# A decoder kernel on one core: raw scores that run ahead, moved between the scores of two pairs of heads

## The reference, cut to what matters

```python
# layer 0: head width 8 (weights ternary, inputs quantised, rotary left out here)
att = jnp.einsum('bhnr,bhmr->bhnm', ql, kl) / math.sqrt(dk)
y = jax.nn.softmax(att, axis=-1) @ v
# layer 2: head width 8
scores = jnp.einsum('bnhr,bmhr->bhnm', Qr, Kr) / math.sqrt(RANK)
A = jax.nn.softmax(scores, axis=-1)
out = jnp.einsum('bhnm,bmhv->bnhv', A, V).reshape(b, n, d)
# layer 3, first attention of its cross block: head width 32, masked after the softmax
a = jax.nn.softmax(jnp.einsum('bhsd,bhtd->bhst', q, k) * D ** (-0.5), axis=-1)
mask = (jnp.arange(t)[None, :] > jnp.arange(s)[:, None]).astype(a.dtype)
o = jnp.einsum('bhst,bhtd->bhsd', a * mask, v)
```

## Time and profile before

| | |
|---|---|
| median of 3 runs | 1848.97 us (1846.86 to 1850.07) |
| the profiled execution | 1849.52 us, its span 1846.9 us |
| PE busy | 1549.2 us (84%) |
| DVE busy | 1040.8 us (56%) |
| ACT busy | 643.8 us (35%) |
| POOL busy | 211.0 us (11%) |
| rounds of layer 0's attention, 79.66 to 178.70 | PE 94.72, DVE 76.94, ACT 64.52 busy of 99.04 us, clock 0.96 |
| rounds of layer 2's attention, 1007.85 to 1104.30 | PE 92.13, DVE 76.89, ACT 64.64 of 96.45 us, clock 1.00 |
| rounds of layer 3's attention, 1518.13 to 1648.30 | PE 124.72, DVE 84.44, ACT 70.55, POOL 46.50 of 130.17 us, clock 1.00 |

### The profile page before, as it was taken

One profiled execution on the slowest core, in us unless ns is written; L12 is line 12 of the kernel. 1 busy time (PEld: TensorE's weight loads), 2 busy tenths in 40 slices (PEclk: granted clock), 3 DMA queues, 4 the chain that ended last, 5 costly groups with the idle time before them and its releaser, 6 DMA issues. The chain is left out here.

```text
span 1846.9 us, 22396 instructions
## 1 busy us (share of the span) xinstructions
PE 1549.2 (84%) x8280; PEld 707.8 (38%) x8280; DVE 1040.8 (56%) x2589; ACT 643.8 (35%) x926; POOL 211.0 (11%) x227
## 2 busy tenths in 40 slices
PE   1798689995677999988989998988988679996986
PEld 0332344442233344446433333353446423344343
DVE  4696445447945677753444962535445457734444
ACT  1366242214324033333424663412221255542431
POOL 2000010001000524331000000000000103321000
PEclk9899689996979889998998997997996789997798
DMA  4000000002000000000020000000010000000000
GB/s 200 0 1 1 1 1 0 1 26 108 1 0 1 17 29 2 1 1 1 1 88 13 1 1 0 1 1 1 1 68 1 1 0 1 2 1 1 1 1 12
DMA packets 4075, 27.16 MB, mean 15 GB/s; under 512 B 384, under 2 KB 2432, under 8 KB 2944
## 3 DMA queue, kind: packets, MB, share of 16 engines
q1 hardware_dynamic: 2912, 25.22, 3.4%
q10 hardware_dynamic: 1056, 0.52, 0.1%
HBM read 25.21 MB, written 0.52 MB: 14 GB/s over the span
## 5 line engine op out<-in xcount | busy, mean ns | idle before, releaser
L792 DVE TENSOR_REDUCE maxima<-banks 128x1 f32<-128x512 f32 (+4 forms) x640 | 362.7, 603 | 103.5 <-PE banks L647 96.4
L929 ACT ACTIVATE big<-banks 128x1024 f32<-128x1024 f32 (+2 forms) x320 | 294.3, 960 | 262.4 <-PE banks L690 94.1
L675 PE MATMUL banks<-big 32*128 32x512 f32 (+6 forms) x1280 | 230.3, 607 | 17.0 <-DVE big L813 12.6
L647 PE MATMUL banks<-big 32*128 32x77 bf16 (+6 forms) x1024 | 157.4, 293 | 22.9 <-ACT big L238 6.1
L1390 DVE TENSOR_TENSOR big<-big,banks 128x512 f32<-128x512 f32 (+1 forms) x116 | 79.7, 687 | 151.5 <-PE banks L1303 146.1
L711 PE MATMUL banks<-big,v_heads 128*9 128x512 f32 (+7 forms) x1024 | 158.6, 565 | 6.3 <-ACT heads_out L852 3.2
L446 POOL TENSOR_TENSOR rstd<-mean_var,minus_half 128x4 f32<-128x4 f32 x34 | 34.5, 1014 | 1078.8 <-DVE mean_var L346 1078.8
L1365 ACT ACTIVATE big<-banks 128x512 f32<-128x512 f32 (+1 forms) x116 | 69.1, 596 | 178.1 <-PE banks L1302 178.0
L647 PEld LDWEIGHTS banks<-big 32*128 32x128 bf16 (+1 forms) x1024 | 57.1, 97 | 177.3 <-DVE maxima L792 90.8
L1333 PE MATMUL banks<-big,moe_weights 128*128 128x512 f32 (+1 forms) x232 | 118.9, 597 | 3.0 <-ACT big L1373 2.6
L336 DVE BATCH_NORM_STATS2 stats<-banks 128x6 f32<-128x128 f32 x128 | 28.5, 284 | 135.6 <-PE banks L324 135.6
(11 more groups left out here) (409 smaller groups left out, 2254.6 us busy)
## 6 DMA issues: line engine op xcount, KB each, us to landing
moe_weights<-in_moe SPq DMA_DIRECT2D x1, 4864.0 KB, 14.9
moe_weights<-in_moe SPq DMA_DIRECT2D x1, 4768.0 KB, 22.0
moe_weights<-in_moe SPq DMA_DIRECT2D x1, 3264.0 KB, 10.5
moe_weights<-in_l3x SPq DMA_DIRECT2D x1, 3072.0 KB, 10.0
late_weights<-in_l2x SPq DMA_DIRECT2D x1, 2048.0 KB, 8.0
moe_weights<-in_l SPq DMA_DIRECT2D x1, 1234.0 KB, 13.1
rows<-in_rows SPq DMA_DIRECT2D x1, 1152.0 KB, 8.0
late_weights<-in_turned SPq DMA_DIRECT2D x1, 1152.0 KB, 17.3
```

What stands on the lines that cost most here:

```text
L647: last = nc.tensor.matmul(RING[n % NR][:, x * klen:x * klen + last_key(t)], q[rows, t * P:(t + 1) * P], ks[rows, 0:last_key(t)], start=Tru ...
L675: last = nc.tensor.matmul(SC[pair % 2][0:size, j % 2, n0:S], ks[rows, i * P:i * P + size], q[rows, n0:S], start=True, stop=turned)
L792: nc.vector.tensor_reduce(dst, src, AX_X, ALU.max).then_inc(ring_free.up(), 1)
L929: nc.scalar.activation(E[pair % NEP][0:size, :, n0:S], SC[pair % 2][0:size, :, n0:S], ACT.Exp, scale=scale).then_inc(exp_ready.up(), 1)
```

## The change

`scores` can now issue one pair alone, and where there are two pairs and more than one key tile, raws 0 and 1 stand between pair A's scores and pair B's. Everything else keeps its place.

```diff
--- before.py
+++ after.py
@@ -660,14 +660,15 @@
             last = nc.tensor.transpose(to[:, t * P:(t + 1) * P], negmax_tile, unit[:])
         last.then_inc(ring_ready.up(), 1)
 
-    def scores(pe, r):
+    def scores(pe, r, half=None):
         g, i = r // nkt, tile(r)
         b, k = groups[g]
         size, n0 = key_tiles[i], start(i)
         q, ks = queries(b, k), keys(b, k)
         if r % nkt == 0:
             pe.wait_ge(ring_free.sem, ring_free.at(maxima_turned[g] + 1))
-        for j in range(HB):
+        heads = range(HB) if half is None else range(2 * half, 2 * half + 2)
+        for j in heads:
             pair = r * pairs + j // 2
             if j % 2 == 0 and pair >= 2:
                 pe.wait_ge(exp_ready.sem, exp_ready.at(pair - 1))
@@ -675,7 +676,7 @@
             last = nc.tensor.matmul(SC[pair % 2][0:size, j % 2, n0:S], ks[rows, i * P:i * P + size], q[rows, n0:S], start=True, stop=turned)
             if turned and j % 2:
                 last.then_inc(score_ready.up(), 1)
-        for j in range(0 if turned else HB):
+        for j in () if turned else heads:
             pair = r * pairs + j // 2
             rows = slice(W * j, W * j + W)
             last = nc.tensor.matmul(SC[pair % 2][0:size, j % 2, n0:S], c.pick[rows, 4 // HB * j, 0:size], c.NMT[rows, g % 2, n0:S],
@@ -880,12 +881,15 @@
                 pe.wait_ge(project_free.sem, project_free.at(len(projections)))
             for r in range(R + later):
                 soon, rest = ahead(r)
+                between = pairs == 2 and nkt > 1
                 if r < R:
-                    scores(pe, r)
+                    scores(pe, r, 0 if between else None)
                 turn_first = mask == "causal" and next_group(r) is not None
                 if not turn_first:
                     for u in soon:
                         raw_scores(pe, u)
+                if r < R and between:
+                    scores(pe, r, 1)
                 if 0 <= r - 1 < R:
                     values(pe, r - 1)
                 if next_group(r) is not None:
```

## The result

The changed kernel took 1896.95 us, the median of four executions (1890.91 to 1898.54); the kernel before, measured beside it, 1848.54 (1846.86 to 1850.07). The ratio is 1.0256, with a 95% interval of 1.0231 to 1.0281: slower by 48.4 us, where 46.2 were forecast. The profiled execution is the lowest of the four, 1890.91 us with a span of 1888.0.

The account below looks back on a forecast made before the run. The prediction took the matmul engine's in-order chain, from pair A through pair B to the values, as the bound. Row-8 stages 28.4 plus layer 3 17.8 gave 46.2 us more, 1895.2 us, range 1877 to 1908.

Parts of the forecast that it names:

- The wait and its length: Row-8 rounds: pair B can't start before raw 1's weight load, 0.61, 1.18, 1.18 and 1.34 us after pair A.
- Values pass it on in full: Row-8 group: each delay of pair B reaches the values and the next round undiminished, 2.13 us a group, 14.49 for 12.36.
- 9.2 us less: Row-8 stages: lower bound if unseen slack swallowed the short delays of rounds 0 and 1, 14 x 0.66.
- Layer 3: Self-attention with a ring of two banks: rounds longer by 0.24, 0.85, 0.62 and 0.86 us, 17.8 in all.
- Ring banks: Longer rounds: reductions don't gate them, since banks for raws 2 and 3 are free earlier than wanted.
- Strict order: Rival, chance 0.14: pair B starts only with the held raws before it in PE's queue; 9.2 us more, 1904.4.
- the sum that hung on it, 55.4: Loss in us over the three stages instead of 46.2, if matmuls start and end strictly in program order.
- No hold: Rival, chance 0.06: pair B's products pass a raw waiting for its bank, so pair B starts as now; 1849 us.
- The repeated wait: The only instruction added, a wait already met; the forecast gave it no cost.
- took every group for a steady one: The sum applied one steady group's delays to all rounds with raws ahead: 28.4 us row-8, 17.8 layer 3.
- The place behind pair B costs the raws nothing: Old order: raws wait for pair A's rows, 0.96 us, longer than pair B's wait; gain booked at 0.
- the "faster" rival: Rival, chance 0.04: the vector engine is fed earlier in the row-8 stages, up to 14.0 us won, 1835.

Follow-up runs that it names:

- wait_only: Kernel before, order kept; ahead of pair B's first product PE waits for the bank raw 1 will take: 1893.37 us, 1.0259.
- no_repeat: Changed kernel without the repeated wait for the turned maxima ahead of pair B in a group's first round: 1893.42 us, 1.0246.
- after_again: The changed kernel run and profiled once more, nothing altered: 1898.33 us, 1.0267 against the kernel before.
- raw0_row8: Against the changed kernel: only raw 0 between the pairs, raw 1 behind pair B, and this in the row-8 stages alone: 1859.48 us, 1.0056.
- row8_only: Against the kernel before: the new order in the two row-8 stages alone, not in layer 3: 1880.12 us, 1.0182.
- l3_only: Against the kernel before: the new order in layer 3's first attention alone: 1865.73 us, 1.0106.
- raw0_between: Against the changed kernel: only raw 0 between the pairs, raw 1 behind pair B, in all three stages: 1862.20 us, 1.0075.

## Why the prediction was right

**The wait and its length.** The central step was that pair B can't start before raw 1's weight load, 1.18, 1.18 and 1.34 us after pair A in three rounds of four. The profile after has 1.17, 1.18 and 1.34, and wait_only pays the same with the wait alone (47.7 us in its stages, against 48.0 and 46.0).

**Values pass it on in full.** In a steady group this holds. The four rounds of a row-8 group got longer by 0.48, 0.27, 0.74 and 0.73 us; the forecast was 0.38, 0.28, 0.74 and 0.73. The group took 14.58 us where 14.49 was forecast. Nothing was swallowed by slack there, for which the prediction had named 9.2 us less.

**Layer 3.** The rounds got longer by 0.18, 0.97, 0.64 and 0.86; the forecast was 0.24, 0.85, 0.62 and 0.86. The stage lost 17.5 us for 17.8.

**Ring banks.** That the reductions would not gate the longer rounds holds in this group: the weights of raws 2 and 3 load at 127.20, 130.42 and 134.22, within 0.01 us of pair A's start. DVE's busy time stayed (11.33 us before, 11.26 after) and its share fell.

**Strict order.** This rival is wrong. In the first round the first two passes of pair B start ahead of the raws that stand before them in the queue: the row of six at 124.46, the raws at 125.43. Had pair B started with the raws, it would have been 0.97 behind pair A and the group some 0.36 us longer than forecast; the first round was 0.10 longer than forecast, and for another reason (below). By the Trainium skill (TensorE: Matmul & The Clock Gate, Part 3, "The mechanism") matmuls are in program order in start and in end; for starts this trace doesn't agree, here as in the earlier trace rows, and the sum that hung on it, 55.4, didn't come.

**No hold.** Wrong too: in the three rounds of this group in which raw 1 waits, pair B's loads come 0 to 0.01 us behind raw 1's, never ahead.

**What was mis-sized.** The repeated wait was booked as nothing. It costs 0.1 us in the first round of each group, on the path there because pair B decides: 0.7 us over the seven groups of a stage, some 2 us in all. no_repeat shows 2.1 (43.9 in the stages against 46.0). In the forecast of the group this is the whole difference between 14.49 and 14.58.

**What cancelled it.** The sum also took every group for a steady one. The first isn't: in layer 2's stage (after_again) its rounds got longer by 0, 0.14, 0.73 and 0.49 us, 1.37 in all, where the forecast had 2.13. In layer 3 the first two groups lost 1.90 and 2.45 us, where the steady ones lost 2.65 and the forecast had 2.57. Without the repeated wait, in no_repeat, the stages lost 43.9 us, so the forecast of 46.2 for that same mechanism was 2.3 too high. A term put at nothing and a term put too high, some 2 us each, met in 46.0: that is luck.

**What was overlooked.** "The place behind pair B costs the raws nothing" is right for their start and wrong for their report. In the kernel before, in the round of the earlier trace rows whose raws start at 134.34:

```profile
134.34 0.61 PE L647 MATMUL banks<-big 32*128 32x512 bf16 x2
...
134.81 0.59 PE L675 MATMUL banks<-big 32*128 32x512 f32 x2
...
135.49 2.55 DVE L792 TENSOR_REDUCE maxima<-banks 128x1 f32<-128x512 f32 x4 [0.40 <-PE banks L647]
```

Raw 0 takes about 0.4 us, so it ended near 134.74; DVE, idle, took it at 135.49, 0.09 after pair B's last pass (134.81 + 0.59). In the new order DVE starts 0.42 us after the raws' start, at 125.85 and at 1594.67. raw0_row8 moves this raw ahead of pair B and nothing else in the round, with pair B again 0.90 us behind pair A, and the idle time is gone. One row holds all six reductions, the four before the raw's and two more:

```profile
121.32 3.80 DVE L793 TENSOR_REDUCE maxima<-banks 128x1 f32<-128x512 f32 x6 [0.24 <-PE banks L647]
```

So the "faster" rival had a mechanism, which I had taken for absent. It gained nothing there: no round of raw0_row8's group is shorter than before, and one is longer. It shows once the wait is paid in both orders, in layer 3 of wait_only, in the round whose pair A starts at 1573.85:

```profile
1575.18 0.39 PE L649 MATMUL banks<-big 32*128 32x512 bf16 x2
...
1575.90 0.38 PE L686 MATMUL banks<-negmaxT,pick 32*128 32x512 bf16 x2
...
1576.35 1.29 DVE L799 TENSOR_REDUCE maxima<-banks 128x1 f32<-128x512 f32 x2 [0.94 <-PE banks L649]
...
1577.19 0.38 PE L663 MATMUL banks<-ident_bf,negmax 128*128 128x128 bf16 x4 [0.56 <-DVE maxima L799]
```

The raws, queued behind pair B here, start at 1575.18 and are taken at 1576.35, 0.07 after pair B's last product (1575.90 + 0.38). The transposes of the maxima (L663, L660 in the other kernels) wait 0.56 us for that reduction and come 3.34 after pair A; in the changed kernel they came 2.61 after it, with no such wait. The round takes 5.33 us instead of 4.62. Six such rounds are 4.3 us; less the 0.7 of the repeated wait, which wait_only doesn't have, that is the difference of the stages, 3.5 us (148.1 against 144.6). That is what the new order gives: 3.5 of 21.0 us in layer 3. In the row-8 stages nothing of the kind is seen (+13.4 and +13.3 against +14.4 and +14.1 with the repeated wait).

**The total.** 46.2 us were forecast for the stages; they lost 48.0 in one profile and 46.0 in the other. 2 of the 48.0 are the clock at the start of layer 2's stage. The medians, 48.4 and 50.0 us over the kernel before, hold a few us more than the 46.0; code outside the stages took 1528.6, 1521.7 and 1532.1 us in three profiles. Of the 3.5 us between the first and the last, 3.1 lie between layer 2's stage and layer 3's: 415.9 us before, 419.0 in after_again and in row8_only, at a granted clock of 0.86 instead of 0.87. Whether the new order brings this lower clock isn't shown; the first profile of the same order has 416.5 there. That the total came within 2 us of the forecast is partly luck; that a steady group did within 0.1 is not.

## What to carry to other kernels

When an instruction is moved ahead in an in-order queue, its wait moves with it: look first at what stands behind it, and at the latest moment at which its wait has ever been met. In these traces a product on free rows overtook one whose rows were taken, but none passed a wait. Here a place one step earlier bought a report some 0.7 us sooner and held the next pair until 1.34 us behind the first, which cost up to 0.74 us a round in the row-8 stages and 0.97 in layer 3; if work must go there, what has to be found first is a free bank, not a free slot. And when a sum is made from one steady group, the first groups of a stage want a look of their own.

## What the runs showed of the hardware

**Starts and reports are in different orders.** A product may start ahead of one before it in the queue when that one's rows are taken (the first passes of pair B ahead of the raws at 125.43). Its end was told to another engine only behind the end of what stood ahead of it in the queue: a raw that ended near 134.74 was taken at 135.49, and in wait_only's layer 3 one that ended near 1575.57 was taken at 1576.35. With the raw ahead of pair B the delay was gone (raw0_row8). The second half agrees with what the Trainium skill (TensorE: Matmul & The Clock Gate, Part 3, "The mechanism") says of ends, that they come in program order.

**A wait already met is not free, where it is a second one on the path.** The traces of the changed kernel have 22417 instructions, those of the kernel before and of no_repeat 22396. The 21 are the repeated waits, one in each of seven groups in three stages (row8_only has 14 of them, l3_only 7): a second wait ahead of one weight load is an instruction of its own. It cost 0.1 us a group. It doesn't cost that everywhere: wait_only has 78 instructions more than the kernel before (22474), and its group is as short as no_repeat's, 14.47 us.

**Code that isn't touched moves by several us.** Outside the stages the instructions are the same in every kernel here. The windows between layer 0's and layer 2's stage, of the two profiles of the changed kernel:

```profile
190.50:1014.80 824.30, 700.11 (x3244) 321.29 (x3239) 478.51 (x1157) 258.11 (x404) 122.23 (x112) 0.92 0.04 16
```

```profile
191.70:1023.10 831.40, 711.17 (x3244) 326.41 (x3238) 478.53 (x1157) 258.32 (x404) 122.26 (x112) 0.89 0.04 16
```

Seven us lie between a mean granted clock of 0.92 and one of 0.89, and only PE is busier (711 us against 700). The mean clock doesn't settle the length to better than some 3 us: this stretch took 828.2 us in no_repeat and 831.0 in raw0_between, both at 0.90. Nor is it only chance between executions, as raw0_row8 shows. So what an edit does to its own stages is read in these stages here, and the total can differ from that by some 7 us, in either direction.
